# Two-block attention kernel: three bias matmuls of a step become rows that ScalarE copies into the banks, and the t product is issued ahead of the low parts

## What is computed

```
style = s @ aff_w.T + aff_b                      # one row per batch
w_mod = w * style * rsqrt(sum((w * style)**2) + 1e-8)
kx = x @ w_mod_k.T + k_b                         # 16 heads of 32
A = softmax(kx_h . kx_j / sqrt(32)) over the 16 heads of the same token
x = x + (A @ kx) @ w_mod_o.T + o_b
```

```
h = LN(LN(x, pw_g[path], pw_b[path]), cp_g[comp], cp_b[comp])
t = LN(x, tm_g[time], tm_b[time]);  s = LN(x, ms_g[scale], ms_b[scale])
m, n, r = x + mlp_ln(memory), x + mlp_ln(noise), x + mlp_ln(resource)
cat = [w0*h, w1*t, w2*m, w3*n, w4*r, w5*s]       # w = softmax(aw)
x = x + LN(silu(cat @ int_W1 + int_b1) @ int_W2 + int_b2, int_g, int_be)
```

## Time and profile before

| | |
|---|---|
| median of 3 runs | 938.13 us (935.24 to 938.22) |
| the profiled execution | 936.79 us, span 935.0 us |
| busy share of the span: PE, DVE, ACT, POOL | 94%, 75%, 48%, 63% |
| mean granted TensorE clock | 0.968 |
| steps 7, 8, 9, from z_T to z_T | 55.10, 54.20, 50.84 us |

### The profile page before, as it was taken

How to read it: one execution, slowest core, us unless ns; L and a number is a source line. 1 busy time by engine, 2 the same in 40 slices (tenths; PEclk the granted TensorE clock), 3 DMA queues, 4 the chain that set the end, 5 groups by cost and what they waited for, 6 DMA issues and landing times.

```text
span 935.0 us, 19902 instructions
## 1 busy us (share of the span) xinstructions
PE 876.8 (94%) x7518; PEld 789.8 (84%) x7566; DVE 698.0 (75%) x1129; ACT 450.6 (48%) x790; POOL 592.5 (63%) x742
## 2 busy tenths in 40 slices
PE   5876798999999999999999999999999999999987
PEld 5744697988989898998989898998979898999886
DVE  3679867778697777778787777778787777768642
ACT  3565336454544546454544645454544645453421
POOL 2267797766566675756576675856676675857551
PEclk9987799999999999999999999999999999999999
DMA  8951232422333232323334242323334242222110
GB/s 291 414 203 33 70 97 69 119 56 93 97 110 111 81 108 68 108 54 104 99 91 130 69 119 69 90 50 116 102 84 122 68 117 64 93 53 85 35 46 23
DMA packets 101871, 93.78 MB, mean 100 GB/s; under 512 B 72720, under 2 KB 75024, under 8 KB 100112
## 3 DMA queue, kind: packets, MB, share of 16 engines
q1 hardware_dynamic: 91984, 67.93, 24.0%
q0 software_dynamic: 4608, 16.78, 6.5%
q10 hardware_dynamic: 5184, 7.79, 2.7%
HBM read 67.83 MB, written 8.39 MB: 82 GB/s over the span
## 4 chain that ended last, share of the span: by engine, by line
PE 50%; DVE 26%; issue 9%; ACT 7%; another core or an unknown queue 4%; POOL 2%; DMA 2%; ACTq 1%; DVEq 0%; SPq 0%; POOLq 0%
PE acc L368 30%; PE tok L368 12%; PE att L368 3%; PE xp L511 3%; PE xp L368 2%; DVE norm L1280 2%; DVE ytmp L1266 2%; DVE SE L1195 2%; DVE small L1199 1%; DVE SE L1222 1%; DVE SE L1210 1%; DMA p_kb<-in_kb 1%; ACT pgb L795 1%; DVE alo L1228 1%
## 5 line engine op out<-in xcount | busy, mean ns | idle before, releaser
L1476 POOL TENSOR_TENSOR xlo<-xraw,xhi 128x512 fp32r<-128x512 f32 x32 | 46.8, 1464 | 104.8 <-ACT xhi L736 104.8
L1530 POOL TENSOR_TENSOR op1l<-ytmp,op1h 128x512 fp32r<-128x512 f32 x64 | 84.2, 1316 | 31.1 <-ACT op1h L824 30.7
L368 PE MATMUL acc<-op1h,W1th 128*128 128x256 f32 x256 | 80.2, 313 | 10.9 <-POOL op1l L1530 10.9
L368 PE MATMUL acc<-op0h,W1xh 128*128 128x256 f32 x256 | 77.2, 301 | 1.5 <-DVE op0l L1252 1.5
L824 ACT CAST op1h<-ytmp 128x512 fp32r<-128x512 f32 x64 | 39.7, 621 | 78.6 <-DVE ytmp L1266 78.6
L368 PE MATMUL acc<-op1h,W1hh 128*128 128x256 f32 x256 | 77.5, 303 | 0.0
L368 PE MATMUL acc<-op1l,W1th 128*128 128x256 f32 x256 | 77.4, 302 | 0.0
L368 PE MATMUL acc<-op1h,W1tl 128*128 128x256 f32 x256 | 77.3, 302 | 0.0
L368 PE MATMUL acc<-op0h,W1sh 128*128 128x256 f32 x256 | 73.7, 288 | 0.0
L368 PE MATMUL acc<-op0h,W1xl 128*128 128x256 f32 x256 | 73.0, 285 | 0.0
L368 PE MATMUL acc<-op0l,W1xh 128*128 128x256 f32 x256 | 73.0, 285 | 0.0
(11 more groups left out here) (248 smaller groups left out, 3201.2 us busy)
## 6 DMA issues: line engine op xcount, KB each, us to landing
xsq<-in_x SPq DMA_DIRECT2D x32, 256.0 KB, 4.3
xb<-in_x SPq DMA_DIRECT2D x32, 256.0 KB, 2.9
out<-xb SPq DMA_DIRECT2D x32, 256.0 KB, 2.0
xraw<-in_xT SPq DMA_DIRECT2D x31, 256.0 KB, 4.3
BD<-q SPq DMA_DIRECT2D x124, 64.0 KB, 2.1
BD<-v SPq DMA_DIRECT2D x124, 64.0 KB
ring<-in_k_wT ACTq DMA_DIRECT2D x12, 256.0 KB
ring<-in_o_wT ACTq DMA_DIRECT2D x12, 256.0 KB
```

Source lines behind the costliest of these rows:

```text
L368: return e.matmul(o, a, b, start=start, stop=True, skip_group_check=True)
L1476: e.tensor_tensor(xlo[:, :, :], xraw[:, :, :], xhi[:, :, :].bitcast(F32), ALU.subtract).then_inc(s["xlo"], 1)
L1530: e.tensor_tensor(op[slot]["l"][:, :, half(g)], four(ytmp[YT[n, g][0]]), op[slot]["h"][:, :, half(g)].bitcast(F32), ALU.subtract).then_inc ...
```

## The change

The rows of k_b and int_b2 lie in SBUF (`kb`, `b2`, one copy on each partition, loaded in the opening). ScalarE copies them into the bank before the matmuls, which then all accumulate. bias_q does that for the k projection of even tiles from 4 on; the other k projections keep their bias matmul. bias_2 does it for all of W2. The waits that guarded the banks move from TensorE to these copies, and TensorE waits for the copies (`sd`, `sw`). `GT` and gain_tables go: the gains matmuls read 32 partitions of `tab` (0 to 31 for t, 32 to 63 for s, 96 to 127 for h) and the same 32 of the one-hot rows. In steps with batch weights z_copy stands ahead of mod_hi on ScalarE, and product(pb,"t") ahead of mod_lo on VectorE. demod(0,1) and demod(1,1) move from steps 1 and 2 into GpSimd's opening. Three semaphores of the second-layer weights become one.

```diff
@@ -462,25 +462,30 @@
                 mm(Pp[quad(2), :], cst[:, 24:56], rv[0][:, :], start=True).then_inc(s["Pm"], 1)
 
             def proj(g, kts=range(4)):
+
                 o = tok[1 if g else 0]
-                if kts[0]:
-                    pass
-                elif g == 0:
-                    e.wait_ge(s["c_one"], 48)
-                    e.wait_ge(s["tq"], 1)
-                elif g > 1 and g % 2 == 0:
-                    e.wait_ge(s["ql"], g)
-                elif g > 3:
-                    e.wait_ge(s["w"], g - 3)
-                elif g == 3:
-                    e.wait_ge(s["ql"], 3)
-                e.wait_ge(s["xlo"], g + 1)
+                on_bias = g > 3 and g % 2 == 0
+                if kts[0] == 0:
+                    if g == 0:
+                        e.wait_ge(s["c_one"], 48)
+                        e.wait_ge(s["tq"], 1)
+                    elif on_bias:
+                        e.wait_ge(s["sd"], g // 2 - 1)
+                    elif g == 2:
+                        e.wait_ge(s["ql"], 2)
+                    elif g > 3:
+                        e.wait_ge(s["w"], g - 3)
+                    elif g == 3:
+                        e.wait_ge(s["ql"], 3)
+                    e.wait_ge(s["xlo"], g + 1)
                 for kt in kts:
                     if g % 8 == 0:
                         e.wait_ge(s["mwl"], 8 * (g // 8) + kt + 1)
-                    three(o[:, :], xhi[:, kt, :], xlo[:, kt, :], WL["k", "h"][:, kt, :], WL["k", "l"][:, kt, :], kt == 0)
+                    i = three(o[:, :], xhi[:, kt, :], xlo[:, kt, :], WL["k", "h"][:, kt, :], WL["k", "l"][:, kt, :], kt == 0 and not on_bias)
                 if kts[-1] == 3:
-                    mm(o[:, :], selT[:, 0, :], tab[:, :]).then_inc(s["A"], 1)
+                    if not on_bias:
+                        i = mm(o[:, :], selT[:, :], tab[:, :])
+                    i.then_inc(s["A"], 1)
 
             def scores(g):
                 if g:
...
@@ -548,9 +553,10 @@
                 if g % 2 == 0:
                     e.wait_ge(s["oh"], g // 2 + 1)
                 if g == 0:
-                    e.wait_ge(s["G"], "tsh".index(n) + 1)
+                    e.wait_ge(s["tq"], 1)
+                q = quad({"t": 0, "s": 1, "h": 3}[n])
                 for c in range(4):
-                    i = mm(o[:, c * 128:c * 128 + 128], GT[n][:, c * 128:c * 128 + 128], OH[(g // 2) % 2][:, half(g)], start=(c == 0))
+                    i = mm(o[:, c * 128:c * 128 + 128], tab[q, c * 128:c * 128 + 128], OH[(g // 2) % 2][q, half(g)], start=(c == 0))
                 i.then_inc(s["G" + n], 1)
 
             def W1_part(k, n, pair, js=(0, 1)):
...
@@ -580,28 +586,17 @@
                         i.then_inc(s["W1" + n], 1)
 
             def W2_part(g, ms):
+
                 o = tok[g % 2]
+                if ms[0] == 0:
+                    e.wait_ge(s["sw"], g + 1)
+                    if g == 0:
+                        e.wait_ge(s["wlp"], 4)
                 e.wait_ge(s["asl"], 2 * (g // 2) + ms[0] // 2 + 1)
                 for m in ms:
-                    three(o[:, :], op[0]["h"][:, m, half(g)], op[0]["l"][:, m, half(g)], WL["2", "h"][:, m, :], WL["2", "l"][:, m, :], m == 0)
-
-            def W2_first(g):
-                if g < NG - 2:
-                    if g % 2 == 0:
-                        e.wait_ge(s["x1"], g + 3)
-                    elif g + 3 < NG:
-                        e.wait_ge(s["ql"], g + 4)
-                elif g == NG - 2:
-                    e.wait_ge(s["x1"], NG)
-                else:
-                    e.wait_ge(s["w"], NG - 2)
-                if g == 0:
-                    e.wait_ge(s["wlp"], 4)
-                W2_part(g, (0, 1))
-
-            def W2_last(g):
-                W2_part(g, (2, 3))
-                mm(tok[g % 2][:, :], selT[:, 1, :], tab[:, :]).then_inc(s["W2"], 1)
+                    i = three(o[:, :], op[0]["h"][:, m, half(g)], op[0]["l"][:, m, half(g)], WL["2", "h"][:, m, :], WL["2", "l"][:, m, :], False)
+                if ms[-1] == 3:
+                    i.then_inc(s["W2"], 1)
 
             style(0)
             demodulation(0)
...
@@ -677,14 +672,14 @@
                 if front:
                     gains(a, "t")
                     u_T(a)
-                W2_first(pa)
-                W2_first(pb)
-                W2_last(pa)
+                W2_part(pa, (0, 1))
+                W2_part(pb, (0, 1))
+                W2_part(pa, (2, 3))
                 if front:
                     a_T(b)
                 if more:
                     scores(a + 2)
-                W2_last(pb)
+                W2_part(pb, (2, 3))
                 if front:
                     out_proj(b)
                     x_T(a)
...
@@ -746,6 +741,23 @@
                 if g:
                     e.wait_ge(s["qT"], g)
                 e.activation(qt[:, :, 0], tok[1 if g else 0][:, :], ACT.Copy, scale=inverse(g)).then_inc(s["qh"], 1)
+
+            def bias_q(g):
+
+                e.wait_ge(s["ql"], g)
+                e.copy(tok[1][:, :], kb[:, :]).then_inc(s["sd"], 1)
+
+            def bias_2(g):
+
+                if g % 2 == 0:
+                    e.wait_ge(s["x1"], min(g + 3, NG))
+                elif g < NG - 1:
+                    e.wait_ge(s["ql"], min(g + 4, NG))
+                else:
+                    e.wait_ge(s["w"], NG - 2)
+                if g == 0:
+                    e.wait_ge(s["c_ob"], 32)
+                e.copy(tok[g % 2][:, :], b2[:, :]).then_inc(s["sw"], 1)
 
             def sum_part(g, of, to):
                 for h in range(2):
...
@@ -877,7 +890,7 @@
             e.wait_ge(s["xlo"], 1)
             e.dma_start(xraw[:, :, :], A["xT"][1]).then_inc(s["ldx"], 16)
             e.wait_ge(s["c_kb"], 16)
-            e.activation(kb[:, :], kb[:, :], ACT.Square, scale=2.0 ** -12, accum_out=sum_b[:, :]).then_inc(s["kbs"], 1)
+            e.activation(kb2[:, :], kb[:, :], ACT.Square, scale=2.0 ** -12, accum_out=sum_b[:, :]).then_inc(s["kbs"], 1)
             squares(0)
             e.wait_ge(s["c_wo"], 16)
             square(1, 0)
...
@@ -950,10 +963,10 @@
                     if k == 1:
                         z_copy(pb)
                     e_first(a)
+                if k > 1:
+                    z_copy(pb)
                 if mod:
                     mod_hi(*mod, (0, 1))
-                if k > 1:
-                    z_copy(pb)
                 prod_hi(pb, "t")
                 if mod:
                     mod_next(*mod, (0, 1))
...
@@ -971,6 +984,8 @@
                         split_x(a + 2)
                         squares(a + 2)
                     prod_hi(pb, "s")
+                    if more:
+                        bias_q(a + 2)
                 prod_hi(pa, "h")
                 if mod:
                     mod_next(*mod, (2, 3))
...
@@ -984,13 +999,18 @@
                     mod_load(1)
                 if front:
                     z_make(a)
+                    bias_2(pa)
                     sum_part(b, "S", "Sc")
                     if more:
                         q_hi(a + 2)
                     exponential(b)
+                    bias_2(pb)
                     if mod_of(k + 1):
                         rows_copy(2 * mod_of(k + 1)[0] + mod_of(k + 1)[1])
                     e_first(b)
+                if not front:
+                    bias_2(pa)
+                    bias_2(pb)
                 silu(k - 1, 0)
                 if front:
                     z_copy(a)
...
@@ -1102,11 +1122,6 @@
                 e.wait_ge(s["c_tab"], 16)
                 e.tensor_scalar(tr[:, :], tr[:, :], small[:, 12:13], None, ALU.mult).then_inc(s["t0"], 1)
 
-            def gain_tables():
-                e.wait_ge(s["tq"], 1)
-                for i, n in enumerate("tsh"):
-                    e.tensor_scalar(GT[n][:, :], tab[:, :], cst[:, 5 + i:6 + i], None, ALU.mult).then_inc(s["G"], 1)
-
             def hidden_add():
                 e.wait_ge(s["m1"], 1)
                 e.wait_ge(s["c_one"], 48)
...
@@ -1368,9 +1382,9 @@
                     finish(pa - 2)
                 if front:
                     e_second(a)
+                product(pb, "t")
                 if mod:
                     mod_lo(*mod, (0, 1))
-                product(pb, "t")
                 if k > 1:
                     finish(pb - 2)
                 v_stats(pb)
...
@@ -1550,6 +1564,8 @@
             demod(1, 0)
             gather(0)
             true_scale(0)
+            demod(0, 1)
+            demod(1, 1)
             for kt in range(4):
                 mod_first_lo(kt)
             x_lo(2)
...
@@ -1611,8 +1627,6 @@
                     add_ob(b)
                     prod_lo(a, "t")
                     gather(b)
-                if k < 3:
-                    demod(k - 1, 1)
                 if more:
                     true_scale(a + 2)
                 root3(pa)
```

30 lines of the change are left out of this document (15 added, 15 removed).

## The result

The changed kernel takes 940.41 us (median of 11 runs, 939.81 to 942.54), the kernel before in the same comparison 936.24 us (11 runs, 934.17 to 938.25). The ratio is 1.0046, 95% interval [1.0034, 1.0058]: 0.46% slower, where 919.2 us was forecast. The profiled execution has a span of 938.3 us, 3.3 us more than the 935.0 of before.

What follows compares the result with a forecast made beforehand. VectorE was taken to set the period between W2(pa) and proj(b), TensorE everywhere else. 936.8 - 7.1 (bias matmuls) - 11.8 (t product first) = 917.9, gains and rest 0; 1.3 higher against the median: 919.2 us, range 909 to 936.

Steps and rivals of the forecast that it cites:

- Gains from 32 partitions: All 96 gains groups on TensorE contract over 32 partitions: 0 us taken, bounds 0 to 0.2 us a group, 19.2 in all.
- the table sum of the earlier trace: Matmuls with 32 output columns, the nearest in kind: 0.1 us in and 0.1 us out, left to a rival.
- The loads of today run ahead: Argument against a weight load of about 0.1 us added to each gains group's 0.2 us.
- Steps with batch weights: Six steps with the t product first: 20.2 us gained without the `op1l` wait and slow clock, 8.4 returned, net 11.8.
- the first return: New TensorE wait of 1.1 us for `alo` at gains(pa,"h") in six batch-weight steps, bounds 0.7 and 1.7 us.
- the chain of b: Attention chain ending in `e_second`: about 1.1 us later, overdrawing 0.5 us of slack by 0.6 in steps 4, 8, 12.
- Bias matmuls: W2 and proj bias matmuls removed from TensorE: 31 count at 0.23 us each, 7.1 us in all.
- the gap before proj(b): TensorE waits there for `w` from VectorE's last_norm(pb); forecast near 0.9 us.
- The copies: 46 ScalarE bias copies into PSUM, nearest row 0.59 us, bounds 0.4 to 0.8: ordinary steps lose nothing.
- Slower: Rival: next full weights can't load until the gains group leaves the array; 0.3 us a group, 948 us, chance 0.10.
- Array switching: Rival: each gains group costs 0.1 to 0.2 us more; 927 to 936 us, say 931, chance 0.31.
- The stall only moves: Rival: the new wait at gains(pa,"h") is 1.7 us and the clock falls behind it; 931 us, chance 0.13.

Runs made afterwards that it cites:

- e1_rows128: Changed kernel with the gains matmuls over all 128 partitions (full height; computation changed): 926.87 us, ratio 0.9898 to the kernel before.
- e2_rows32_alone: Kernel before with only the 32-partition gains added, masked tables still made but not read: 948.62 us, ratio 1.0134.
- e3_order_alone: Kernel before with the order alone: z_copy ahead of mod_hi, product(pb,"t") ahead of mod_lo(0,1): 931.91 us, ratio 0.9945.
- e12_short_xlo: e3_order_alone with GpSimd's low part of x cut from 128 to 8 columns a block in the six batch-weight steps (computation changed): 925.91 us, ratio 0.9872.
- e6_copies_alone: Changed kernel with gains over 128 partitions and the old order of z_copy, mod_hi, product and mod_lo (bias rows alone): 929.60 us, ratio 0.9926.
- e4_rows96: Changed kernel with the gains matmuls over 96 partitions instead of 32 (computation changed): 928.00 us, ratio 0.9915 to the kernel before.
- e10_scalar_too: e7_k_weights_late plus, in steps 3, 7, 11, ScalarE's a_hi(a) ahead of u_make(pb) and split_x ahead of mod_hi(2,3): 931.10 us, ratio 0.9936.
- e7_k_weights_late: e3_order_alone with VectorE's mod_weights(2,3) and mod_lo(2,3) moved later in steps 3, 7, 11: 929.39 us, ratio 0.9925.
- e11_best: e3_order_alone plus ScalarE's W2 bias copies, keeping the k projection's bias matmul and 128-partition gains: 928.67 us, ratio 0.9911.
- e5_rows64: Changed kernel with the gains matmuls over partitions 0 to 63 for all three tables (computation changed): 940.41 us, ratio 1.0044.

## Why the prediction was wrong

The sum had 18.9 us less than before; the span has 3.3 us more, a miss of 22.2 us. It falls into two terms.

**Gains from 32 partitions: the step that failed.** I took 0 out of bounds of 0 to 0.2 us a group, "the row of the same instruction in size and type". Measured: 0.25 us. In the nine ordinary steps, 54 groups, that is 13.4 us; those steps, the opening and the tail together came out 13.8 us above the sum (9.4 us more than before, where 4.4 us less was forecast). That the two figures are so near is partly chance: the opening's 1.6 us more and the 1.6 us of clock in step 15 stand against each other in it. The groups' price itself rests on the ordinary steps of e1_rows128 and e2_rows32_alone. The row I chose says what such a matmul costs among its like; the one I set aside, the table sum of the earlier trace rows, showed the crossing: 0.1 us in and 0.1 out, near the 0.09 and 0.13 measured here. And it was no upper end: its two sides were read to 0.01 us from one place, and the weight load that can no longer run ahead was priced in the rival and left out of the bounds. "The loads of today run ahead" was true and argued the wrong way: what ran ahead was what could be lost.

**Steps with batch weights: a term mis-sized.** Forecast were 11.8 us and the 12 bias matmuls that lie in these steps, 14.6 us; measured 6.1. The mechanism was right up to the first return: no wait for `op1l`, clock at 1.00, a wait for `alo` of 0.8 us on the average and 1.3 at most (forecast 1.1), the chain of b 0.3 us late in step 8 (0.6). What was missing: I noted that the low parts run against GpSimd, but charged it only to `alo`. In the order alone mod_lo(2,3) came to 3.18 us from 1.28, and a second wait of 0.56 us at u_T or out_proj stood behind the first. In the changed kernel the waits of the six steps add up to 6.2 us (`alo` 4.8, `Wol` 1.1, `e` 0.3), less than the 8.4 us that the sum returned; at full height they are 10.2 (7.0, 1.7, 0.3, and 1.2 at u_T). What TensorE pays for the groups there, it waits less. Nor did all of the 3.36 us a step come back: in the order alone 0.37 us of step 7 stand in no wait row and stay open. (The window of the earlier trace rows that the prediction calls step 9 runs from 531 to 582 us; over step 9 itself, 536.66 to 587.50, the granted clock is 1.00 as well.) The order alone, the changed kernel and the one with full height need 321.8, 321.8 and 322.0 us for the six steps. Whether TensorE has 12 bias matmuls less or pays for 36 gains groups hardly shows in them; that VectorE, with GpSimd beside it, sets them is what e12_short_xlo supports.

**Bias matmuls: right.** 0.43 us less in an ordinary step (0.46), and the gap before proj(b) at 0.91 us (0.9). The 6.8 us of the run with the bias rows alone (7.1) agree in part by chance, as said there.

**The copies: right.** 0.58 us each, no wait for them, ordinary steps untouched.

**The rivals.** "Slower" named the right mechanism: the load of the next full weights starts only with the matmul behind the group. Its price was 0.3 us and is 0.25. Its point of decision, 0.2 us a group over all 96, was made against the full gain of the other terms; the true balance is 13.4 us lost in ordinary steps against 6.1 us won in the others and 4.4 us of bias matmuls. "Array switching" had the place right and the price too low. "The stall only moves" didn't come in the changed kernel, but in a single step of each of four other runs: in e1_rows128 TensorE waits 2.0 us for `alo` in step 7, the clock over that step is 0.97, and it takes 55.07 us where steps 3 and 11 took 53.73; the same in step 8 of e4_rows96 (54.16), step 12 of e10_scalar_too (54.60) and step 3 of e12_short_xlo. In step 4 of e7_k_weights_late, step 12 of e11_best and step 7 of e12_short_xlo the wait is 2.0 us too and the clock 1.00.

## What to carry to other kernels

Before a matmul is cut to fewer rows, look at its neighbours: between full-array matmuls each crossing, into a 64- or 32-row shape or back out of it, cost 0.11 to 0.12 us of TensorE here, which no wait row shows, so that six short groups (1.49 us a step) more than paid away the 0.43 us that three removed bias matmuls had brought. Bound an unknown cost by what the nearest row of the same *transition* shows, not by the row of the same instruction. And when work is moved on VectorE, look at what GpSimd does at the new place: an instruction's duration belongs to its neighbours as much as to itself. Last, before a total is taken as agreement, go through the steps that the edit leaves alone: here one of them moved by 1.6 us with the clock.

## What the runs showed of the hardware

- Crossing between the full array and 64 or 32 rows: 0.23 us (64 rows, e5_rows64) to 0.25 us (32 rows, e1_rows128 and e2_rows32_alone) for a pair around a group of four bf16 matmuls of 128 columns; the weight load no longer starts 0.11 us ahead. 96 rows cost nothing (50.45 us a step for 50.41).
- Two VectorE subtractions over 512 columns with both inputs in SBUF: 1.28 us with GpSimd mostly idle (before), 2.11 with a part of its work taken away (e12_short_xlo), 3.18 beside two GpSimd subtractions (e3_order_alone). GpSimd's own xlo took 1.75 us in that stretch, and 1.28 in step 7 of the changed kernel, where the two of VectorE took 2.28.
- A ScalarE copy of a whole bank from SBUF into PSUM: 0.58 us.
- TensorE's granted clock over a step with batch weights: with an idle time of 1.2 to 1.3 us in it 1.00 (all six of e2_rows32_alone; steps 3, 7 and 11 of the changed kernel), with 1.7 us 0.97 in all six steps of the kernel before but only in three of six in e6_copies_alone. With 2.0 us it is 0.97 in four steps and 1.00 in three. The same idle time doesn't always bring the fall.
